# One order of work changed: the first FFN of a two-layer transformer kernel on one core

## The reference

```
h = layernorm(x) * (1 + ca) + sa;  x = x + ga * attention(h)
h = layernorm(x) * (1 + cb) + sb;  x = x + gb * ffn(h)
```

## Time and profile before

| what | before |
|---|---|
| median of 3 runs | 1528.65 us |
| profiled execution, time | 1520.89 us |
| profiled execution, span | 1519.1 us |
| PE busy, share of the span | 1390.8 us, 92% |
| DVE busy | 1186.1 us, 78% |
| ACT busy | 1033.9 us, 68% |
| POOL busy | 344.4 us, 23% |

### The profile page before, as it was taken

The page is one execution under the profiler, slowest core; times in us unless marked ns, Lnnn a source line. Parts: engine busy times, 40 slices in busy tenths (PEclk is TensorE's granted clock), DMA queues, the critical chain, the costliest instruction groups (busy, mean ns, idle before and its releaser), DMA issues. The chain is left out here.

```text
span 1519.1 us, 35666 instructions
## 1 busy us (share of the span) xinstructions
PE 1390.8 (92%) x13548; PEld 584.6 (38%) x13548; DVE 1186.1 (78%) x1530; ACT 1033.9 (68%) x1976; POOL 344.4 (23%) x472
## 2 busy tenths in 40 slices
PE   6888898999899899996999999999999999989998
PEld 3543333333333255441233333333333333236665
DVE  6686797888796044899999979997999789717766
ACT  3254676777688833221899989998999889964443
POOL 2501130300100033124140028301400040055225
PEclk9997899999999999997899999999999999999999
DMA  7821120111000003223200200000000000012454
GB/s 227 162 35 40 47 72 25 38 33 50 1 2 2 1 15 71 49 39 65 91 7 7 54 7 7 7 7 6 7 7 7 7 2 2 5 67 88 143 156 145
DMA packets 56868, 68.53 MB, mean 45 GB/s; under 512 B 9819, under 2 KB 52379, under 8 KB 55963
## 3 DMA queue, kind: packets, MB, share of 16 engines
q1 hardware_dynamic: 53635, 57.87, 14.7%
q0 software_dynamic: 3072, 8.39, 1.8%
HBM read 45.26 MB, written 26.74 MB: 47 GB/s over the span
## 5 line engine op out<-in xcount | busy, mean ns | idle before, releaser
L1854 DVE TENSOR_REDUCE mpart<-psum 128x2 f32<-128x1024 f32 (+2 forms) x832 | 913.0, 1157 | 91.8 <-PE psum L1265 74.0
L1582 ACT ACTIVATE probs<-psum 128x512 f32<-128x512 f32 (+1 forms) x1512 | 771.9, 573 | 157.2 <-PE psum L1301 84.2
L1326 PE MATMUL psum<-probs,v_region 128*17 128x256 f32 (+1 forms) x6400 | 502.9, 387 | 18.6 <-ACT probs L1576 9.3
L1265 PE MATMUL psum<-key_region,row_region 50*128 50x512 f16 (+3 forms) x1664 | 323.3, 381 | 46.8 <-DVE mpart L1854 36.7
L1301 PE MATMUL psum<-row_region,key_region 52*128 52x512 f16 (+3 forms) x1664 | 341.5, 380 | 17.6 <-ACT probs L1582 11.9
L1301 PEld LDWEIGHTS psum<-row_region,key_region 52*128 52x128 f16 x1664 | 93.9, 93 | 335.8 <-ACT probs L1582 264.4
L1326 PEld LDWEIGHTS psum<-probs,v_region 128*17 128x17 f32 x6400 | 107.1, 95 | 220.8 <-issue 114.3
L1060 POOL TENSOR_SCALAR mp<-mx 128x16 f16<-128x16 f32 x32 | 10.3, 322 | 647.7 <-DVE mx L1865 617.3
L1265 PEld LDWEIGHTS psum<-key_region,row_region 50*128 50x128 f16 x1664 | 94.8, 94 | 149.2 <-DVE mpart L1854 85.6
L1576 ACT ACTIVATE probs<-psum 128x1024 f32<-128x1024 f32 (+3 forms) x76 | 69.7, 955 | 11.0 <-PE psum L1301 8.5
L1617 ACT ACTIVATE probs<-psum,gate_s 128x512 f32<-128x512 f32 (+1 forms) x24 | 16.4, 682 | 64.9 <-PE psum L1369 64.9
(11 more groups left out here) (196 smaller groups left out, 1358.8 us busy)
## 6 DMA issues: line engine op xcount, KB each, us to landing
parts<-key_region SPq DMA_DIRECT2D x32, 256.0 KB, 3.0
key_region<-parts SPq DMA_DIRECT2D x48, 128.0 KB, 4.3
sorted_x<-in_zero SPq DMA_DIRECT2D x46, 128.0 KB, 2.6
key_region<-sorted_x SPq DMA_DIRECT2D x46, 128.0 KB
sorted_y<-key_region SPq DMA_DIRECT2D x46, 128.0 KB
row_region<-parts SPq DMA_DIRECT2D x144, 32.0 KB
key_region<-in_wmod SPq DMA_DIRECT2D x2, 1536.0 KB, 11.6
x_sb<-in_x SPq DMA_DIRECT2D x4, 512.0 KB, 8.3
```

What stands on the lines that cost most here:

```text
L1265: mm = pe.matmul(bank(b + par)[:, 0:w], rows[at, g, hp, r * P:(r + 1) * P], keys[at, g * HP + hp, q * CH:q * CH + w], start=True, stop=not ...
L1326: mm = pe.matmul(psum[32 * h:32 * h + VW, SUM_BANK, lo:hi], v_sb[:, jt, g * HG + h, :], probs[:, (S0[y] + s) % 2, h, lo:hi], start=(jt == ...
L1582: nc.scalar.activation(probs[:, (S0[y] + s) % 2, 2 * hp + par, off:CH], psum[:, e % 3, off:CH], ACT.Exp, scale=SCALES[y]).then_inc(s_p, 1)
L1854: V.tensor_reduce(mpart[:, n % NG, at:at + 2, q:q + 1], psum[:, b:b + 2, 0:w], AX.X, ALU.max).then_inc(drained(*item)[0], 1)
```

## The change

- Chunk 0's six pairs are run with only `ft` and `bt` between them; `oq` and `op` stand behind the sixth, and then at once chunk 0's down product and statistics, ahead of chunk 1's first pair.
- In chunk 1's pairs (tc = 1) `nm` of chunk 0 stands behind pair 0, `ln` and the last attention chunk's `st` behind pair 1, the projection of the keys and their load behind pair 2, that of the rows and their load behind pair 3, the last attention chunk's `ln` behind that, and the values behind pair 5, with one block right after them.
- So `loaded` is 1 from the start of chunk 2's pairs; stage 2 holds 56 blocks in place of 52.
- Two blocks fewer stand between `mt` and the first scores of the second attention.
- In the last part `nm` and `ln` of chunk 3 stand ahead of the values of chunk 2, and one block is moved out.
- The last key chunk is loaded in two parts (heads of the first group, the other heads), those of even heads by SP, those of odd heads by ACT, behind the last values; the first group waits for its own semaphore `s_last`.
- The first maxima (y = 1, n = 0) are placed by two DMAs of SP and two of ACT.
- The two constant DMAs of the second layer's first rows are issued before SP waits for the stored parts.

```diff
-    first = 6 if todo[0] else 0
-    out = todo[0] + [("mp", y, 0)] + todo[1][:2] + [("mt", y, 0), ("place", y, 0)] + todo[1][2:6] if todo[0] else []
+    first = 4 if todo[0] else 0
+    out = todo[0] + [("mp", y, 0)] + todo[1][:2] + [("mt", y, 0), ("place", y, 0)] + todo[1][2:4] if todo[0] else []
...
     for c in range(NC[0]):
-        out.extend(hidden_pair(0, 0, c) + (tail(0, c) if c < 5 else []))
+        out.extend(hidden_pair(0, 0, c) + (tail(0, {0: 0, 1: 1, 5: 2}[c]) if c in (0, 1, 5) else []))
+    out += [("dn", 0, 0, 0), ("sa", 2, 0), ("dn", 0, 0, 1), ("st", 2, 0)]
...
+            if tc == 1:
+                out += {0: [("nm", 2, p)], 1: [("ln", 2, p)] + tail(0, 3)}.get(c, [])
+                if c == 2:
+                    project_keys(p, 1)
+                    out += tail(0, 4)
+                if c == 3:
+                    project_rows(p, 1)
+                    out += tail(0, 5)
+                if c == 5:
+                    out.append(("v", 1, p))
+                    loaded[0] = 1
+                    blocks(1)
+                continue
...
-    out.append(("st", 2, p))
     loaded[0] = p
+    out += [("st", 2, p), ("qk", 1, p - 1, 0), ("nm", 2, p), ("ln", 2, p), ("ql", 1, p - 1, 0)]
     blocks(1)
-    out += [("qk", 1, p - 1, 0), ("nm", 2, p), ("ql", 1, p - 1, 0), ("v", 1, p - 1), ("ln", 2, p)]
-    blocks(4)
+    out.append(("v", 1, p - 1))
+    blocks(3)
     project_keys(p, 1)
     project_rows(p, 1)
-    out.append(("v", 1, p))
+    out += [("v", 1, p), ("keys odd", 1, p)]
     blocks(7)
...
+        def load_last_keys(engine, par):
+            tok = slice(T - CH, T)
+            for heads, landed in ((slice(0, HP), s_last), (slice(HP, H // 2), s_key[NCH - 1])):
+                for k, part in enumerate(COL_PARTS):
+                    src = parts[1, part, :, tok].rearrange("(h r c) t -> r c h t", r=2, c=HD)[par][:, heads, :]
+                    lo = 64 * par + C0 + HD * k
+                    engine.dma_start(keys[lo:lo + HD, heads, tok], src).then_inc(landed, 16)
...
             def load_first_rows(y):
+                if y:
+                    sp.wait_ge(s_e, HG * S0[1])
+                    first_row_constants(y)
                 sp.wait_ge(*parts_stored(y, 0, 0))
-                if y:
-                    first_row_constants(y)
...
+                if y and q == NCH - 1 and g == 0:
+                    pe.wait_ge(s_last, 96)
+                else:
+                    pe.wait_ge(s_key[q], 96 * (y + 1))
...
+                if item[1:] == (1, 0):
+                    act.wait_ge(*drained(*item))
+                    for h in range(HP, HG):
+                        lo = 64 * (h % 2) + M0
+                        nc.scalar.dma_start(rows[lo:lo + 2, 0, h // 2, :], mrow_t[32 * h:32 * h + 2, :]).then_inc(s_mrow, 16)
```

More of the change, by code:

```diff
@@ L312, in ffn0_walk @@
                 out.append(("st", 2, p))
[L313 to L316, removed]
+            if c == 2:
                 out.append(("nm", 2, p))
-            if c == (2 if tc == 1 else 3):
+            if c == 3:
                 out.append(("ln", 2, p))
             if c == 5:
-                if tc > 1:
-                    project_keys(p, 1)
+                project_keys(p, 1)
                 if tc < NCH - 1:
@@ L666, in adaln_two_layers @@
         s_key = [sem(f"keys_loaded{q}") for q in range(NCH)]
+        s_last = sem("last_keys_of_first_group_loaded")
         s_rows = sem("first_chunk_rows_loaded")
@@ L863, in load_keys @@
                     sp.wait_ge(s_e, HG * S0[1])
+                if (y, q) == (1, NCH - 1):
+                    load_last_keys(sp, 0)
+                    return
                 tok = slice(q * CH, (q + 1) * CH)
@@ L872, in place_maximum @@
                 sp.wait_ge(*drained("mt", y, n))
-                for h in range(HG):
+                for h in range(HG if (y, n) != (1, 0) else HP):
                     lo = 64 * (h % 2) + M0
@@ L1258, in max_pair @@
                 pe.wait_ge(*rows_loaded(y, n))
-                pe.wait_ge(s_key[q], 96 * (y + 1))
+                if y and q == NCH - 1 and g == 0:
+                    pe.wait_ge(s_last, 96)
+                else:
+                    pe.wait_ge(s_key[q], 96 * (y + 1))
                 pe.wait_ge(s_kc, 64)
@@ L1589, in copy_maximum, with odd_keys @@
                 nc.scalar.activation(mrow_t[:, :], bank(bank_of(item)), ACT.Identity).then_inc(drained(*item)[0], 1)
+                if item[1:] == (1, 0):
[3 more added lines that the diff above has]
+                        nc.scalar.dma_start(rows[lo:lo + 2, 0, h // 2, :], mrow_t[32 * h:32 * h + 2, :]).then_inc(s_mrow, 16)
+            def odd_keys(item):
+                act.wait_ge(*parts_stored(*item[1:], 1))
+                load_last_keys(nc.scalar, 1)
             def copy_out(item):
@@ L1673, in _ @@
                     copy_out(it)
+                elif it[0] == "keys odd":
+                    odd_keys(it)
                 elif it[0] == "bt":
```

## The result

The changed kernel takes 1545.72 us (median of 4 runs, 1542.06 to 1546.48) against 1528.79 us before on the same chip: a ratio of 1.0123, 95% interval 1.0099 to 1.0146. It is slower by 16.9 us where +10.4 was forecast; the median is at the upper end of the range (by the ratio, 1.0123 x 1528.65 = 1547.5, just beyond it) and outside the 1535 to 1542 of the likeliest case. It lies in the range only because the range took in the spread of the runs: the sum's own bounds were +3.1 to +14.1.

The account below looks back on a forecast made before the run. PE and DVE were both full in the second attention; the first block waited on a DMA chain. Terms +7.4, +2.7, +1.5, -1.0, +0.9, 0 and -1.1 summed to +10.4 us, giving 1539.0 us; range 1530 to 1546.

Parts of the forecast that it names:

- likeliest case: The forecast itself for the whole kernel, with its own spread of 1535 to 1542 us; chance 0.68.
- term 1: First block behind chunk 0's values: PE stands still until the rows land, +7.4 us (+4.6 to +7.4).
- term 2: Behind the first block's wait: PE's clock at half for 3 to 7 us, +2.7 us (bounds 1.5 to 3.5).
- term 3: Five more blocks in chunk 2's part cost +1.5 us; four fewer in the attention stage give -1.0 us.
- term 4: Chunk 3's norm ahead of chunk 2's values: the key projection ends 0.9 us later (-0.5 to +1.5).
- term 5: End of stage: last keys' load in two parts hidden, 0; placing on two queues saves issues, -1.1 us (0 to -1.3).
- Rival 1: First block behind the values: the rows are there in time; -0.8 us, 1527.9 us; chance 0.12.
- Rival 2: Behind the first block's gap: half clock lasts longer, 12 us costing 6; +13.7 us, 1542.3 us; chance 0.08.
- Rival 3: Smaller stall, chain bound by the rows' store; attention regains its blocks' whole price; +5.6 us, 1534.3 us; chance 0.12.

Follow-up runs that it names:

- e7: Changed kernel with half of chunk 0's second-layer keys not loaded; the first block's wait was 4.54 us; one execution, no ratio.
- e2: Changed kernel, placing still on two queues, but the second FFN's weights held back until the placing has landed; ratio 1.0066 to the kernel before.
- e1: Changed kernel with the first maxima placed by four DMAs of SP again, none by ACT; ratio 1.0067 to the kernel before.
- e10: Kernel before with only the placing of the first maxima on two queues, SP and ACT; ratio 1.0007.
- e6: Changed kernel with placing on SP and first block late again, plus normalisation of chunks 1 and 2 one pair earlier; ratio 1.0006 to the kernel before.
- e12: Kernel before with only the normalisation of chunks 1 and 2 one pair earlier; ratio 0.999.
- e9: Changed kernel with placing, first block and chunk 3's norm undone, earlier normalisation, three blocks behind the last values, an older block before chunk 2's row projection; ratio 0.9962.
- e11: e9 with the last keys loaded whole by SP alone, waited for once; ratio 1.0002 to the kernel before.

## Why the prediction was wrong

The direction was right, and so was the largest term. By the profiles E is 18.6 us later, which is about what the ratio gives (0.0123 x 1528.79 = 18.8 us).

| step | forecast | measured | from |
|---|---|---|---|
| up to the values of chunk 0 | 0 | -0.7 | 53.0 against 53.7 us from the start |
| term 1, wait of the first block | +7.4 | +6.2 | 7.24 - 1.09 |
| term 2, clock behind it | +2.7 | +2.9 | half of 5.8 us at 0.50 under load (0.57 over 591.3 to 598) |
| term 2, two more falls | 0 | +3.4 | 621 and 665, 1.7 each |
| term 3, blocks in chunk 2 | +1.5 | +1.7 | what is left to the values of chunk 1 |
| term 4, chunk 3's norm | +0.9 | +1.1 | what is left to M |
| term 5, placing | -1.1 | +3.8 | 8.56 - 4.76 |
| term 3, attention | -1.0 | +0.3 | S to E |

What is left, for example: from the values of chunk 0 to those of chunk 1 there were 41.8 us and are 54.3; of the 12.5 the wait took 6.2, the half clock 2.9 and 1.7, and 1.7 stay for the blocks. In e7, with the same list, the same reckoning leaves 1.9.

**The step that failed is term 5**: "With two on each queue two issues go: -1.1 us (0 to -1.3)." The sum counted what the edit removes from SP's queue and not what moves up when two issues go. Behind them stood the weights' load of 3.5 MB, and with SP free 1.2 us earlier it was issued ahead of ACT's second placing, whose packets then moved some 4.7 us behind their issue (731.3 to 736.0) and 1.2 us in e2. The result was +3.8 at S, 4.9 us from the forecast and outside its bounds; e1, e2 and e10 show it from both sides. The earlier trace rows holds the placing's row and not the load behind it.

The page that I weighed there gives the reason in part. By the Trainium skill (DMA: Bandwidth & Descriptors, Issuing engines are not separate DMA queues) the second queue saves the time of issue alone; e2's 0.4 us agrees. The same page (Queues, rings and completion order, HWDGE ordering) says that the write that signals a DMA's end lands behind every earlier write of that DMA engine, across its queues. That would let a transfer of 2 KB be reported as late as the bulk around it. The packets show that most of the delay here is another: the placing's own data moved late, at 736.0 and 736.5, and its signals followed within 0.3 us of each. So the transfer itself began late, while the shared engines carried the bulk (share 0.95 at 733 to 742), and not only the report of its end. In what way the bulk held it back is open.

**Term 1 was right, its size a little high.** The cause (a chain that hangs on the keys' transfers, the engines full) was the one forecast, and e7 confirms it. From the end of the keys' low parts (571.43 + 0.74) to the block 19.2 us passed, where I had 21.6 - 1.35 = 20.2. That is most of the 1.2 us by which the term was too high. That the block ran at 591.32 and not at 594.4 is mostly something else: this execution reached the stage 1.3 us sooner, and the values lay 0.7 sooner in it.

**Term 2 was right for the gap, and had no place for the later falls.** Behind the gap the clock was at 0.50 for some 10 us, 5.8 of them under load, in my bounds. The two later falls, behind transposes that wait 1.37 us for DVE and then 0.64 more, were in no term; at 3.4 us they are the second largest part of the miss. e6 has neither the waits nor the falls. But e10 shows the falls in the order before as well, and e7 shows the changed order without them, so they can't be put down to the change: the profile I added my terms to was one without them. What share of the 16.9 us they are is open.

**Term 3 in the attention** gave back less than forecast. The raw stretches S to E mislead, since the profiles of before and of after each have one fall of the clock late in it, with PE full and some 1.7 us lost, that the others below don't have (first row before, second after; columns as in the windows above):

```profile
1227.90:1231.30 3.40, 3.40 (x25) 0.50 (x24) 1.68 (x2) 2.22 (x5) 3.09 (x5) 0.50 0.00 0
...
1245.70:1249.10 3.40, 3.40 (x26) 0.62 (x23) 2.28 (x2) 2.17 (x4) 3.06 (x5) 0.50 0.00 0
```

Without that fall the fourteen blocks took 585.1, 585.3 and 585.1 us (before, e10, e12) and the ten blocks 585.4, 583.8 and 584.3 (after, e1, e2). The full clock came back 9.4, 8.1 and 8.9 us behind the scores, and 10.1, 7.0 and 7.3. Counting half of these differences, all to 9.4, gives 585.1 to 585.9 against 585.0 to 585.3. So the estimate from these rows is 0 to 0.9 us given back, where -1.0 was forecast. That two blocks fewer ahead of the scores are worth nothing was right: M to S is 4.77 in e1 and 4.76 before.

**The rivals.** Rival 1: the rows were not in time. Rival 2: some 12 us at half clock did come (5.8, 3.4 and 3.4), but not as one longer stretch behind the gap; two of the three are new falls, one of them in chunk 3. Rival 3: the wait lay between its 5.7 us and my 8.5, but e7 speaks against its mechanism, and the attention gave back little. None held a mechanism at the placing. (By its own terms the lowest value of rival 1 is 1526.6 and not 1526.)

**The signs.** The first block's wait of 7 to 9 us came (7.24), and so did the half clock from the middle of the gap and the 2 us of idle time ahead of chunk 3's transpose (2.30 us). The key projection came 3.3 us sooner in the stage, where 2.6 was forecast. The first scores, forecast 1 us sooner behind the copy of the maxima, came 3.8 us later: this sign failed, with term 5.

## What to carry to other kernels

When DMAs leave a queue, look up what stands behind them: it starts earlier by their time of issue, and if it is bulk it can be issued ahead of the last of what was meant to be sped up. Compare the times of issue across both queues. Small transfers on which an engine waits go ahead of the bulk, in its queue or by a wait on their end. Pulling work ahead of its data pays only where the cover over the transfer allows it; and a faster load pays only if the cover over it is cut at the same time (three blocks for seven, e9 and e11).

## What the runs showed of the hardware that I had not expected

- A 2 KB placing on ACT's queue, issued 0.1 us behind a 3.5 MB load on SP's, moved its packets 4.7 us behind its issue, and 1.2 us with the load held back (e2). The three placings issued ahead of the load were not late. The scores came 3.6 to 4.2 us later for it (M to S 8.39 against 4.76; 8.56 against 4.38).
- ACT issued its two placings 1.5 us apart, SP its own 0.65 us.
- A store issued behind 2.7 us of loads on its own queue took 6.0 us until the load waiting for it was issued, and 3.8 with half the loads.
- Gaps of 1.13 and 0.64 us with a transpose between them were followed by 3.4 us at 1.2 GHz in e10, and not in the profile of before, which had the same gaps. Over all profiles 13 of 18 such places were followed by a fall. One profile doesn't tell whether such a fall is there.
